# SBUF tiles at multiples of 512 bytes, and a router product in four passes instead of six

## The reference

```
x = x + tanh(g_xattn[0]) * long_convolution(ctx, ctx, norm(x))
x = x + tanh(g_ffn[0])   * moe0(norm(x))     # 1024 shared hidden, 8 experts of 128, top 2, SwiGLU
x = x + tanh(g_xattn[1]) * causal_attention(norm(x), ctx, ctx)     # 16 heads of 16
x = x + tanh(g_ffn[1])   * moe1(norm(x))     # 256 shared hidden, 32 experts of 128, top 6 by groups, squared ReLU
```

```
scores = sigmoid(x @ router_w.T)                 # moe0: 8 experts
s      = sigmoid(x @ Wr.T + br)                  # moe1: 32 experts
```

## The kernel before

| tile | read by | rest by 512 |
|---|---|---|
| `x_hi_first`, `x_lo_first` | PE, moving, L690 and L374 | 480 |
| `x_hi_last`, `x_lo_last` | PE, moving, L690 and L374 | 32 |
| `y_hi`, `y_lo` | PE, moving, L726 | 288 |
| `w_hi`, `w_lo` | PE, stationary | 288 |
| `k_blocks`, `q_split_t`, `xn_split`, `ident_r` | PE, attention | 32 |
| `toeplitz`, `pair_products`, `weighted` | PE, context stage | 288 |
| `ident` | PE, moving operand of the transposes | 192 |

## Time and profile before

### The profile page before, as it was taken

One profiled execution on the slowest core, in us unless ns is written; L12 is line 12 of the kernel. 1 busy time (PEld: TensorE's weight loads), 2 busy tenths in 40 slices (PEclk: granted clock), 3 DMA queues, 4 the chain that ended last, 5 costly groups with the idle time before them and its releaser, 6 DMA issues.

```text
span 888.7 us, 13950 instructions
## 1 busy us (share of the span) xinstructions
PE 868.7 (98%) x4780; PEld 710.9 (80%) x4780; DVE 587.0 (66%) x1218; ACT 532.9 (60%) x914; POOL 141.4 (16%) x125
## 2 busy tenths in 40 slices
PE   7999999999999999999999899999999999999997
PEld 7998887787788888877777677777788888888886
DVE  4998754565745656599998775658655465556664
ACT  3334443444643444567796766767777877777774
POOL 7996200010112110023231400000000000000000
PEclk9999999999999999999999999999999999999999
DMA  8230333435333432034333054444444344444433
GB/s 281 106 123 27 96 89 101 121 107 187 97 104 118 141 127 68 20 99 122 117 111 100 13 172 137 128 128 143 143 143 125 114 127 149 147 147 147 142 119 107
DMA packets 68389, 106.44 MB, mean 120 GB/s; under 512 B 9120, under 2 KB 31936, under 8 KB 67936
## 3 DMA queue, kind: packets, MB, share of 16 engines
q1 hardware_dynamic: 68112, 105.47, 37.8%
q10 hardware_dynamic: 208, 0.09, 0.0%
HBM read 96.79 MB, written 8.74 MB: 119 GB/s over the span
## 4 chain that ended last, share of the span: by engine, by line
PE 84%; DVE 8%; DMA 2%; issue 2%; POOL 2%; ACT 1%; SPq 1%; DVEq 0%; ACTq 0%; POOLq 0%
PE bank L690 38%; PE bank L726 29%; PE bank L1563 3%; PE bank L1574 2%; PE bank L374 1%; PE bank L1198 1%; PE bank L1199 1%; PE bank L1464 1%; PE bank L1554 1%; DVE max L1754 1%; PE bank L1548 1%; DVE y L1760 1%; PE bank L1217 1%; PE bank L1583 1%; PE bank L355 1%
## 5 line engine op out<-in xcount | busy, mean ns | idle before, releaser
L487 ACT ACTIVATE y_hi<-y 128x512 fp32r<-128x512 f32 x200 | 124.0, 621 | 79.7 <-DVE y L570 79.0
L584 DVE TENSOR_TENSOR y<-y,gate_rows 128x512 f32<-128x512 f32 x124 | 85.7, 691 | 121.2 <-ACT y L476 118.5
L726 PE MATMUL bank<-y_hi,w_hi 128*128 128x512 f32 x400 | 157.3, 393 | 1.9 <-DVE y_lo L320 1.5
L726 PE MATMUL bank<-y_lo,w_hi 128*128 128x512 f32 x400 | 156.6, 391 | 0.0
L726 PE MATMUL bank<-y_hi,w_lo 128*128 128x512 f32 x400 | 155.9, 390 | 0.0
L320 DVE TENSOR_TENSOR y_lo<-y,y_hi 128x512 fp32r<-128x512 f32 x196 | 134.2, 686 | 29.9 <-ACT y_hi L487 29.6
L470 ACT ACTIVATE activated<-bank 128x512 f32<-128x512 f32 x136 | 81.1, 597 | 81.4 <-PE bank L690 76.7
L690 PE MATMUL bank<-x_hi_first,w_hi 128*128 128x512 f32 x264 | 106.2, 402 | 0.7 <-DVE w_lo L315 0.7
L690 PE MATMUL bank<-x_hi_first,w_lo 128*128 128x512 f32 x264 | 104.2, 395 | 0.0
L690 PE MATMUL bank<-x_lo_first,w_hi 128*128 128x512 f32 x264 | 104.1, 394 | 0.0
L690 PE MATMUL bank<-x_hi_last,w_hi 128*128 128x512 f32 x264 | 104.0, 394 | 0.0
(11 more groups left out here) (159 smaller groups left out, 1361.1 us busy)
## 6 DMA issues: line engine op xcount, KB each, us to landing
gate_rows<-gates SPq DMA_DIRECT2D x156, 256.0 KB, 3.7
w_raw<-in_wu SPq DMA_DIRECT2D x68, 256.0 KB, 2.6
w_raw<-in_wu SPq DMA_DIRECT2D x32, 384.0 KB, 4.4
k_blocks<-k_parts SPq DMA_DIRECT2D x128, 64.0 KB, 2.3
k_parts<-xn_split SPq DMA_DIRECT2D x32, 128.0 KB
v_slot<-in_v_rows SPq DMA_DIRECT2D x16, 256.0 KB, 2.9
ctx_windows<-in_ctx_win SPq DMA_DIRECT2D x3, 1024.0 KB, 13.4
x_mixed<-in_x SPq DMA_DIRECT2D x4, 512.0 KB, 8.2
```

The lines of the kernel that those rows point to most:

```text
L487: act.activation(mem.yhi[:, K % S, :], mem.y[:, K % S, :], ACT.Copy).then_inc(s_yh, 1)
L584: dve.tensor_tensor(mem.y[:, K % S, :], mem.y[:, K % S, :], gate, ALU.mult).then_inc(s_yd, 1)
L726: last = pe.matmul(acc(s)[:, c, :], w_[:, Nu % S, wc], y_[:, K % S, :], start=(n == 0 and m == 0), stop=(n == U - 1 and m == 2), skip_grou ...
```

## The change

Two things are changed together.

1. `sb` keeps count of the place in SBUF (`place`, from 16512). Ahead of a tile of 512 bytes and more it takes a gap, so that the tile starts at a multiple of 512. All operands of PE in the table above then have rest 0. The end of SBUF in use moves from 223392 to 226880.
2. The router's high and low weights become one tile `router_split_f0` / `_f1` with 64 columns a feature chunk: 32 high ones, 32 low ones (f0's 8 experts are padded to 32 by the host). `logits_t` multiplies this by `x_hi` and by `x_lo`: 4 passes a block instead of 6. The result has 64 rows: logits by the high weights in rows 0 to 31, by the low weights in 32 to 63. ACT copies 64 rows, the transposes at L387 have 64 columns, and DVE adds the two halves: in f0 a copy and an addition where there was a copy, in f1 two additions where there was one, the second waiting for the first. The product low x low, left out before, is now in the sum.

No instruction is moved past another; the order on every engine is otherwise as before.

```diff
+SBUF_BASE, LINE = 16512, 512
+EG, LG = 32, 64
...
+        place = [SBUF_BASE]
         def sb(name, shape, dt=F32, ctx=top):
+            bytes_ = math.prod(shape[1:]) * (2 if dt == BF16 else 4)
+            gap = -place[0] % LINE if bytes_ >= LINE else 0
+            if gap:
+                ctx.enter_context(nc.sbuf_tensor(f"gap_{name}", [P, gap // 4], F32))
+            place[0] += gap + (bytes_ + 31) // 32 * 32
             return ctx.enter_context(nc.sbuf_tensor(name, shape, dt))
...
-            rwh = sb(f"rwh{tag}", [P, 2, E], F32R)
-            rwl = sb(f"rwl{tag}", [P, 2, E], F32R)
-            lts = mem.lts[0:E]
+            rws = sb(f"router_split_{tag}", [P, 2, LG], F32R)
+            rwh, rwl = rws[:, :, 0:EG], rws[:, :, EG:LG]
+            lts = mem.lts
...
             def logits_t(pe, m, dst):
...
-                i = 0
                 for c in range(2):
-                    for w_, x_ in ((rwh, mem.xh), (rwh, mem.xl), (rwl, mem.xh)):
-                        last = pe.matmul(dst[0:E, :], w_[:, c, :], x_[m // 2][:, c, tok], start=(i == 0), stop=(i == 5))
-                        i += 1
+                    for x_ in (mem.xh, mem.xl):
+                        last = pe.matmul(dst[0:LG, :], rws[:, c, :], x_[m // 2][:, c, tok],
+                                         start=(c == 0 and x_ is mem.xh), stop=(c == 1 and x_ is mem.xl))
...
-                act.activation(lts, src[0:E, :], ACT.Copy).then_inc(s_lc, 1)
+                act.activation(lts[:], src[0:LG, :], ACT.Copy).then_inc(s_lc, 1)
...
-                    last = pe.transpose(dst[:, j * E:(j + 1) * E], lts[:, j * P:(j + 1) * P], ident[0:E, 0:E])
+                    last = pe.transpose(dst[:, j * LG:(j + 1) * LG], lts[:, j * P:(j + 1) * P], ident[0:LG, 0:LG])
...
             def logits(self, dve, src, bs, ready):
-                dve.tensor_copy(self.lg[:, bs, :], src).then_inc(ready, 1)
+                dve.tensor_copy(self.lg[:, bs, :], src[:, :, 0:E0]).then_inc(self.st.sem, 1)
+                self.st.n += 1
+                dve.wait_ge(self.st.sem, self.st.n)
+                dve.tensor_tensor(self.lg[:, bs, :], src[:, :, EG:EG + E0], self.lg[:, bs, :], ALU.add).then_inc(ready, 1)
...
             def logits(self, dve, src, bs, ready):
-                dve.tensor_tensor(self.lg[:, bs, :], src, self.bias[:].unsqueeze(1).broadcast_to((P, BPB, E1)), ALU.add).then_inc(ready, 1)
+                dve.tensor_tensor(self.lg[:, bs, :], src[:, :, EG:LG], self.bias[:].unsqueeze(1).broadcast_to((P, BPB, E1)), ALU.add).then_inc(self.st.sem, 1)
+                self.st.n += 1
+                dve.wait_ge(self.st.sem, self.st.n)
+                dve.tensor_tensor(self.lg[:, bs, :], src[:, :, 0:EG], self.lg[:, bs, :], ALU.add).then_inc(ready, 1)
```

More of the change, by code:

```diff
@@ L12 @@
+import math
 from contextlib import ExitStack
@@ L82, in build @@
         tg = sb("tg", [P, 4])
-        router = {tag: (sb(f"router_{tag}", [P, 2, E]), sb(f"router_bias_{tag}", [P, E])) for tag, E in (("f0", E0), ("f1", E1))}
+        router = {tag: (sb(f"router_{tag}", [P, 2, EG]), sb(f"router_bias_{tag}", [P, E])) for tag, E in (("f0", E0), ("f1", E1))}
         mhalf = sb("mhalf", [P, NB])
@@ L165, in build @@
         mem.xl = [sb("x_lo_first", [P, 2, T // 2], F32R)]
-        mem.lts = sb("logits_t", [E1, BLK])
+        mem.lts = sb("logits_t", [LG, BLK])
         mem.gts = sb("gates_t", [E1, 2, BLK])
@@ L324, in router_hi @@
                 act.wait_ge(s_rl, 64)
-                act.activation(rwh[:].rearrange("p c e -> p (c e)"), rwf[:].rearrange("p c e -> p (c e)"), ACT.Copy).then_inc(s_rw, 1)
+                act.activation(rwh, rwf[:], ACT.Copy).then_inc(s_rw, 1)
             def router_lo(dve):
                 dve.wait_ge(s_rw, 1)
-                dve.tensor_tensor(rwl[:], rwf[:], rwh[:].bitcast(F32), ALU.subtract).then_inc(s_rw, 1)
+                dve.tensor_tensor(rwl, rwf[:], rwh.bitcast(F32), ALU.subtract).then_inc(s_rw, 1)
             def rows_of(m):
@@ L393, in logits_copy @@
                     dve.wait_ge(s_sg, m // 2)
-                rt.logits(dve, src[:, 0:BPB * E].rearrange("p (b e) -> p b e", e=E),
+                rt.logits(dve, src[:, 0:BPB * LG].rearrange("p (b e) -> p b e", e=LG),
                           slice((m % 2) * BPB, (m % 2 + 1) * BPB), s_lgc)
@@ L935, in context_stage @@
             pa = ExitStack()
+            below = place[0]
             NG, NQ = NB // BPB, NB
@@ L1340, in context_stage @@
             pa.close()
+            place[0] = below
             return A
@@ L1878 @@
         "g_x": a["g_xattn"], "g_f": a["g_ffn"], "kpad": kpad, "d_skip": a["L0_xattn_D"],
-        "wu0": np.stack(wu0), "rw0": a["L0_ffn_router_w"].T, "eb0": a["L0_ffn_expert_bias"],
+        "wu0": np.stack(wu0), "rw0": np.pad(a["L0_ffn_router_w"].T, ((0, 0), (0, EG - E0))), "eb0": a["L0_ffn_expert_bias"],
         "wu1": np.stack(wu1), "rw1": a["L1_ffn_Wr"].T, "br1": a["L1_ffn_br"],
```

## The result

| | us |
|---|---|
| before, median of 6 runs | 891.03 (889.90 to 895.65) |
| after, median of 6 runs | 884.68 (882.00 to 890.03) |
| ratio | 0.9924 (95%: 0.9895 to 0.9952) |
| the profiled execution of after | 882.0, of which 880.2 are span |

The change saves 6.4 us of the 29.6 forecast. The direction is right and the time lies in the range. The nearest of the cases is rival B, which forecast 10.5 us less, and that is too much as well: the ratio's interval stands for 4.3 to 9.4 us. B's 882.4 us look closer than they are, since they were taken from a median of before of 892.9 us; from 891.0 they would be 880.5.

What follows compares the result with a forecast made beforehand. PE's passes in f0 and f1 were taken to bound the kernel. Terms of 5.3 + 2.0 + 18.6 + 3.2 + 0.5 = 29.6 us, taken from a median of 892.9, gave 863.3 us; range 848 to 890 us.

Steps and rivals of the forecast that it cites:

- rival B: f0 and f1: only the x_first penalty goes, the floor of 226.7 ns stays; 10.5 us less, 882.4 us; chance 0.27.
- What bounds the kernel: Whole kernel: PE is busy 98% of the span; its 2784 passes in f0 and f1, some 640 us, set the time.
- Term 1: First half of tokens, f0 and f1: aligned x_first passes fall to 226.7 ns, y passes beside them too; 7.3 us.
- Term 2: All 2784 passes of f0 and f1: alignment lowers the floor from 226.7 to 220.0 ns; 18.6 us.
- term 4: Attention: aligned operands make 128 passes and 128 float32r transposes cheaper, partly lost to waiting for DVE; 0.5 us.
- Term 3: Router, eight blocks: four passes for six, less dearer transposes and a wait of PE for DVE's addition; 3.2 us gained.
- Rival A: f0 and f1: all of the excess goes, an aligned pass takes 215.8 ns; 41.7 us less, 851.2 us; chance 0.20.
- Rival C: PE's passes: alignment does nothing, only the router's 3.2 us come; 889.7 us; chance 0.13.
- Rival D: f0 and f1: streams that start level get in each other's way; 4.1 us slower, 897.0 us; chance 0.10.
- My case: Whole kernel: x_first's penalty goes and aligned passes fall to 220 ns; 29.6 us less, 863.3 us; chance 0.30.

Runs made afterwards that it cites:

- w moved: The kernel after with w_hi and w_lo 64 bytes further on, every other large tile at a multiple of 512: 897.7 us, ratio 1.008 to the kernel before.

## Why the prediction was right in direction and wrong in size

**What bounds the kernel** held: PE's passes in f0 and f1. A change of 6.7 ns in all of them moved the whole kernel by 14 us (w moved), one in the 792 passes over x_first and their neighbours by 5.

**Term 1, the x_first passes (7.3 us)**, was right in its steady prices, 226.7 ns for x and y, and too large. Its reason, that an aligned tile is the cheap one, was not the cause: the padding brought x_first level with w, and that it did so is luck. The padding alone saved 0.56 to 0.59%, 5.0 to 5.3 us. The term multiplied all passes by the steady difference; over f0's first half the mean difference was 5.4 ns for x and 2.8 for y, in f1's 4.8 and 3.1 (5.6 and 3.9 from 520 us on). And a wait of 0.2 to 0.8 us for `y_lo` appeared in f0, by the chain behind a gate row's DMA. The prediction named `y_lo` as what could come late, but gave it no price.

**Term 2, the floor (18.6 us)**, is the step that failed: it measured 0. It is 18.6 of the 23.2 us that the forecast was off by the medians. Of the 11.0 us that are left without it 6.4 came (7.4 when after was run again); term 1 accounts for some 2 of what is missing and term 4 for 0.5, and the rest is within the interval. It took the distance of 16 cycles between two prices for a step of a ladder on which alignment goes down one more rung. The two prices are those of two distances between operands, and the cheap one was already the cheapest. The evidence stood in the rows: the passes over x_last and over y cost the same at rests 32 and 288. That a level start costs exactly what another does speaks for a cost without a place in it, and the prediction used it for an upper bound and for rival B, then took a value in the middle, for no reason but the size of a step. One sum was missing: 480 - 288 = 192, 32 - 288 = -256, 288 - 288 = 0. Of three distances two are 0 by 256 and cheap, the third is not and dear.

**Term 3, the router (3.2 us)**, was right: 2.8 us measured alone. Four passes take 0.92 us, as forecast, and PE's second block starts 0.17 us late for 0.25. The transposes with 64 columns take 0.39 us for four, 98 ns each: more than the 85 under which the prediction expected them to stay, 0.4 us in all for the 0.2 taken, and within its bound of 0.8.

**Term 4, the attention (0.5 us)**, came to nothing: 37.3 and 16.9 us before and after. All four operands had rest 32 before, so their distances were 0 already.

**Rival A (851.2 us)** rested on the half-rate rows, which pay 2.5 ns. bf16 passes of one column a cycle pay the same, 216 ns for 512 columns; of the formats measured only float32r pays 13.3. That does not settle whether the rate of reading has a part: by bytes, bf16 at a column a cycle and float32 at a column in two read at the same rate, half that of float32r. What is settled is that no place tried gives any of it back. The Trainium skill ("TensorE: Matmul & The Clock Gate", section "Wait — 56ns, not 53.3ns?") states columns and some 2.5 ns; the bf16 streams agree, the float32r ones at 227 ns do not.

**Rival B (882.4 us)** is what happened in kind, with its reason too: the floor is an excess of the float32r pass that no place tried lowers. Its size, 10.5 us, shares the overrun of term 1 and lies above the interval of 4.3 to 9.4 us.

**Rival C** fell with x_first's gain. The Trainium skill ("SBUF — State Buffer", the box on cachelines under "Door 1: The DMA port swizzle") states a line of 16 bytes. The prediction worked out from it that tiles at multiples of 32 bytes have nothing left to align. This holds in so far as the multiple of 512 earns nothing (883.4 us at rest 288, 883.6 at rest 0); but the distance between two operands, which does not enter that argument, cost 14.1 us.

**Rival D** had the right quantity and the wrong sign. That y and w at one rest cost the floor was held against it, rightly. The same fact, followed on, says that level is cheap, that x_first is the only stream that is not level, and that nothing else is left to win.

**Chances.** My case had 0.30 and B 0.27, with the same sign, so the forecast of a faster kernel held, and the range held because it reached up to C. What was too bold was a point in the middle between a bound of zero and one of 30 us, which no row was near to.

## What to carry to other kernels

When passes of one shape have two prices, list the starts of both operands for each and compare their differences before the places themselves: here the moving and the stationary operand of float32r passes should start at the same rest by 256 bytes, which one small gap does, and any new tile ahead of them can undo (the router's wider tile did, with a third price). A constant excess that is the same at different placements is not a matter of placement; twelve short streams behind a kernel's end tell that in one run. And a saving on the bound engine is worth its steady difference only in unbroken streams, less the waits that it uncovers: look for the transfer that lands just in time.

## What the runs showed of the hardware

- A float32r pass with 128 stationary columns costs its moving columns at 2.4 GHz and 13.3 ns more: 227 ns with 512 columns, 120 with 256. A bf16 pass costs its columns and some 2.5: 216 and 209 ns with 512 and 496.
- On top of that, in a stream whose operands keep their starts, a float32r pass of 512 columns pays for the distance between the start of its moving and of its stationary operand, by 256 bytes: nothing at 0, some 2 ns at 64, 5 to 7.5 ns at 8, 16, 32, 48, 96, 128, 160, 192, 224 and 240, and about 10 at 4 bytes. Where in SBUF the two lay made no difference in the places tried (rests 0, 32, 288 and 480, x_first and x_last). A bf16 stream at a distance of 32 bytes paid nothing. Why this is so was not found. A stream whose places alternate between 0 and 288, each pass level with its own weights, takes 5.59 us for 24 all the same, so a level start of a pass's own two operands is not the whole condition.
- A narrower stationary operand (32 columns for 128) makes a pass dearer, not cheaper: 5.55 us for 24 against 5.48.
- The first passes behind a break in the stream cost more than the steady price (2.98 us for the 12 at f0's start against 2.72), and y passes among dear x passes 230.0 ns where their own price is 226.7.
